# Graph network kernel: four row gathers moved behind four others, and a reciprocal cut into four pieces

## What is computed

```python
h = relu(layernorm(x))                                  # 256 x 1024
feat = concat([h[src], h[dst]], axis=1)                 # per edge, 2048
e_hh = relu(feat[:128] @ W_hh + b_hh)                   # first edges
e_oo = relu(feat[128:768] @ W_oo + b_oo)
e_ho = relu(feat[768:] @ W_ho + b_ho)                   # all other edges
logit = (concat([e_hh, e_oo, e_ho]) @ W_a + b_a)[:, 0]
# softmax of logit over the edges of each dst, then
z = segment_sum(alpha[:, None] * h[src], dst)
x = x + concat([relu([h, z][:64] @ W_hn + b_hn), relu([h, z][64:] @ W_on + b_on)])
# second layer: a 1024 x 1024 matrix, non-zero only in its first 256 x 256
W = zeros(1024, 1024).at[src, dst].add(edge_weight)
return x + relu(layernorm(x)) @ W.T + l1_bias
```

## Time and profile before

| | us |
|---|---|
| median of 3 runs | 326.63 (325.94 to 327.37) |
| profiled execution | 327.02 |
| its span | 325.2 |
| PE busy | 304.7 (94%) |
| DVE busy | 253.2 (78%) |
| ACT busy | 175.9 (54%) |
| POOL busy | 157.0 (48%) |
| DMA | 122.06 MB, mean 375 GB/s |

### The profile page before, as it was taken

How to read it: one execution, slowest core, us unless ns; L and a number is a source line. 1 busy time by engine, 2 the same in 40 slices (tenths; PEclk the granted TensorE clock), 3 DMA queues, 4 the chain that set the end, 5 groups by cost and what they waited for, 6 DMA issues and landing times.

```text
span 325.2 us, 4183 instructions
## 1 busy us (share of the span) xinstructions
PE 304.7 (94%) x1381; PEld 196.4 (60%) x1381; DVE 253.2 (78%) x434; ACT 175.9 (54%) x437; POOL 157.0 (48%) x148
## 2 busy tenths in 40 slices
PE   0899999999999499999999999999999998999995
PEld 0687688845666456656767575666654564366443
DVE  4656445548999199999969989978978979998354
ACT  3854433182467346476884655966219575393202
POOL 3020037405877667757866777538888740000000
PEclk9999999999999969999999999999999999999999
DMA  7999999998999999999999999999999999999604
GB/s 258 406 404 408 366 365 415 409 415 265 342 358 411 410 409 408 410 408 408 411 418 409 409 409 410 408 416 410 408 411 408 410 407 408 408 409 410 231 0 129
DMA packets 34425, 122.06 MB, mean 375 GB/s; under 512 B 4058, under 2 KB 4570, under 8 KB 34404
## 3 DMA queue, kind: packets, MB, share of 16 engines
q0 software_dynamic: 19008, 69.21, 54.1%
q1 hardware_dynamic: 14004, 47.34, 37.6%
q10 hardware_dynamic: 1392, 5.24, 4.0%
HBM read 115.49 MB, written 6.29 MB: 375 GB/s over the span
## 4 chain that ended last, share of the span: by engine, by line
PE 61%; DMA 12%; POOL 11%; DVE 7%; issue 6%; ACT 3%; ACTq 0%; DVEq 0%; POOLq 0%
PE psG L1007 18%; PE psG L865 13%; PE psG L976 9%; DMA Gq<-q_ho,ids 7%; PE psW L915 6%; PE psA L915 5%; POOL Gp L378 5%; POOL Gq L392 5%; DMA q_oo<-T 3%; PE psB L915 3%; PE psG L1084 2%; DVE Gp L681 1%; PE psG L1079 1%; DMA xs<-x 1%; PE psG L876 1%
## 5 line engine op out<-in xcount | busy, mean ns | idle before, releaser
L378 POOL DMA_INDIRECT Gp<-p_ho,ids x60 | 68.2, 1137 | 50.6 <-DMA p_ho<-T 26.3
L392 POOL DMA_INDIRECT Gq<-q_ho,ids x60 | 70.8, 1179 | 34.8 <-issue 17.1
L681 DVE TENSOR_TENSOR Gp<-Gp,Gq 128x1024 f32<-128x1024 f32 x65 | 79.3, 1220 | 10.0 <-DMA Gq<-q_ho,ids 6.8
L1007 PE MATMUL psG<-W,hT 128*128 128x512 f32 x192 | 86.8, 603 | 0.0
L685 DVE SCALAR_TENSOR_TENSOR Gp<-Gp,wa 128x1024 f32<-128x1024 f32 x65 | 79.1, 1217 | 0.4
L1007 PEld LDWEIGHTS psG<-W,hT 128*128 128x128 f32 x192 | 36.2, 194 | 40.2 <-issue 40.2
L489 ACT ACTIVATE RW<-ohs,ewh 128x256 fp32r<-128x256 f32 x66 | 33.2, 503 | 46.8 <-DVE ohs L672 34.4
L915 PE MATMUL psW<-RW,ohd 128*128 128x256 f32 x264 | 44.5, 290 | 1.1 <-issue 1.0
L915 PEld LDWEIGHTS psW<-RW,ohd 128*128 128x128 f32 x264 | 36.3, 189 | 4.5 <-issue 4.3
L915 PE MATMUL psA<-RL,ohd 128*128 128x256 f32 x240 | 35.5, 293 | 3.6 <-issue 2.1
L632 DVE TENSOR_TENSOR Wl<-W,Wh 128x1024 fp32r<-128x1024 f32 x16 | 19.6, 1223 | 21.7 <-ACT Wh L422 21.7
(11 more groups left out here) (180 smaller groups left out, 357.7 us busy)
## 6 DMA issues: line engine op xcount, KB each, us to landing
W<-weights SPq DMA_DIRECT2D x61, 512.0 KB, 13.6
Gp<-weights SPq DMA_DIRECT2D x8, 512.0 KB, 9.9
Gq<-weights SPq DMA_DIRECT2D x4, 512.0 KB, 10.4
pre_f<-weights SPq DMA_DIRECT2D x3, 512.0 KB, 7.9
xs<-x SPq DMA_DIRECT2D x2, 512.0 KB, 3.8
h_rows<-h ACTq DMA_DIRECT2D x1, 1024.0 KB, 6.1
pre_l<-weights SPq DMA_DIRECT2D x2, 512.0 KB, 8.0
p_ho<-T ACTq DMA_DIRECT2D x2, 512.0 KB, 5.4
```

Source lines behind the costliest of these rows:

```text
L378: nc.gpsimd.indirect_dma_start(out=Gp[:, i % NP, :], out_offset=None, in_=p_oo if t <= OO_TILES else p_ho, in_offset=bass.IndirectOffsetOn ...
L392: nc.gpsimd.indirect_dma_start(out=Gq[:, i % NQ, :], out_offset=None, in_=q_oo if t <= OO_TILES else q_ho, in_offset=bass.IndirectOffsetOn ...
L681: nc.vector.tensor_tensor(Gp[:, i % NP, :], Gp[:, i % NP, :], Gq[:, i % NQ, :], ALU.add).then_inc(s_sum, 1)
L1007: last = nc.tensor.matmul(psG[:, 2 * t + half, :], hT[:, k, t * P:(t + 1) * P], W[:, s, half * HALF:(half + 1) * HALF], start=u != 1 and k ...
```

## The change

The order of POOL's first requests was P0 to P11, Q0 to Q7. It becomes P0 to P7, Q0 to Q3, P8 to P11, Q4 to Q7; the rest is as before (Q8, P12, Q9, P13, ...). `few_counts` is no longer called once over 1024 columns ahead of the first row sum; it is called four times, over 256 columns each, after `lot_start(g + 1)` of lots 9, 10, 11 and 12.

```diff
+FEW_LOT = 9
+P_FIRST = 8
@@ gpsimd
-            for i in range(NP):
+            for i in range(P_FIRST):
                 p_rows(i)
-            for i in range(NQ):
+            for i in range(HALVES):
+                q_rows(i)
+            for i in range(P_FIRST, NP):
+                p_rows(i)
+            for i in range(HALVES, NQ):
                 q_rows(i)
             for i in range(NQ, len(GATHERED)):
                 q_rows(i)
@@ vector
-            def few_counts():
+            def few_counts(kind, c):
 
                 dve.wait_ge(s_few, 2)
                 dve.wait_ge(s_wused, SPLIT + 2)
-                chain(nc.vector.tensor_scalar(inv_few[:, :, :, :], few[:, :, :, :], 1.0, None, ALU.max))
-                chain(nc.vector.reciprocal(inv_few[:, :, :, :], inv_few[:, :, :, :]))
-                chain(nc.vector.tensor_scalar(off_few[:, :, :, :], few[:, :, :, :], 0.5, NEG, ALU.is_lt, ALU.mult))
-                chain(nc.vector.tensor_scalar(off_few[:, :, :, :], off_few[:, :, :, :], bar[:, 0:1], None, ALU.add))
+                counts, inverse_of, off_of = few[:, kind, c, :], inv_few[:, kind, c, :], off_few[:, kind, c, :]
+                chain(nc.vector.tensor_scalar(inverse_of, counts, 1.0, None, ALU.max))
+                chain(nc.vector.reciprocal(inverse_of, inverse_of))
+                chain(nc.vector.tensor_scalar(off_of, counts, 0.5, NEG, ALU.is_lt, ALU.mult))
+                chain(nc.vector.tensor_scalar(off_of, off_of, bar[:, 0:1], None, ALU.add))
...
             lot_onehots(0, 0, LOT)
             evac_odd(1)
-            few_counts()
             lot_start(0)
             for g in range(NLOTS):
                 lot_logits(g)
                 lot_start(g + 1)
+                if 0 <= g - FEW_LOT < 2 * NT:
+                    few_counts((g - FEW_LOT) // NT, (g - FEW_LOT) % NT)
```

## The result

The changed kernel takes 331.35 us (median of 4 runs, 329.42 to 332.96), where before takes 327.0 (325.94 to 331.07). The ratio is 1.0126, with a 95% interval of 1.0078 to 1.0174: 4.1 us slower, outside the predicted range. The profiled execution of after took 332.96 us with a span of 331.1. All ratios in this document leave out the executions that fell in a slower state (the traced ones of e10 and e11 among them), and they are formed with executions of before on the same chip, so they need not be the quotient of the two medians.

A forecast was written before the change was run, and what follows sets the result against it. Full DMA engines from about 97 to 301 us were taken as the bound, so the hole before sets the end. Request order +1.3 us and pieces 0, on a median of 326.6, made 327.9 us; range 325.0 to 330.3.

The forecast's parts named there:

- part one: New order of POOL's requests, P8 to P11 behind Q0 to Q3: 1.3 us slower at the end.
- (a): Store of table q_ho lands earlier without P8 to P11 ahead: 3.4 us gained, Q0 asked for at 72.0 us.
- (b): Twelve POOL requests instead of eight ahead of Q8 take 16.3 us: Q8 at 88.3 us, 1.4 us later.
- part two: Counts on DVE in four pieces, 11.8 us added, paid back by its waits: 0 at the end (0 to +3).
- What bounds the kernel: DMA engines full from about 97 to 301 us; the hole before sets the end, if DVE and PE keep up.
- (c): Q8's 1.4 us delay at 369 GB/s leaves 0.52 MB missing, 1.3 us of full DMA to make up behind 97 us.
- (d): DVE's first row sum starts at about 76.7 us, not 80.05; worth nothing, lost in a stop near 114 us.
- The sum: At the end, 1.3 us from the request order and 0 from the pieces: median 327.9 us.
- A: Rival: hole before 97 us filled, Q8 at 85.2 us, 1.7 us earlier; 325.1 us at the end; chance 0.15.
- B: Rival: pieces not paid back, DVE 3 to 4 us late at 262 us; 330.9 us; chance 0.15.
- C: Rival: nothing moves, POOL's gains and losses within 0.5 us; 326.6 us; chance 0.25 together with D.
- D: Rival: PE's slowness around 110 us moves or vanishes; at most some tenths at the end; chance 0.25 with C.

The follow-up runs named there:

- e10: Second set of runs with only POOL's new request order on the kernel before, counts whole at their old place: 329.63 us, ratio 1.0083.
- e11: Kernel before, with P6 to P11 asked for only once the fourth part of the tables has been copied out of PSUM: ratio 1.0007.
- e2: Kernel before with only the counts moved, in four pieces behind lots 9 to 12, old request order: 327.99 us, ratio 1.0035.
- e6: Changed kernel, but with ten P blocks (P0 to P9) ahead of Q0 instead of eight: 329.43 us, ratio 1.0051.
- e9: The changed kernel run again, unchanged: 329.8 us, ratio 1.0111 to the kernel before.
- e5: Changed kernel with the four reciprocals of the counts left out: 330.5 us, ratio 1.0107 to the kernel before.
- e3: Changed kernel, but with only four P blocks (P0 to P3) ahead of Q0: 334.77 us, ratio 1.0279.
- e1: First set of runs with only POOL's new request order on the kernel before, counts whole at their old place: 331.56 us, ratio 1.0176.
- e8: Changed kernel with each of the four reciprocals of the counts made three times: 343.96 us, ratio 1.0494 to the kernel before.
- e4: Kernel before with the counts in four pieces behind lots 14 to 17, old request order: 330.44 us, ratio 1.0121.
- e12: Kernel before with the pieces behind lots 14 to 17 and SP's last four weight loads let go at the 58th row sum, not the 61st: ratio 1.0103.

## Why the prediction was wrong, point by point

The step that failed is the price of part one, and in it two terms: the store's gain (a) and the time of POOL's requests (b). Q8 was to come 1.4 us later and came 3.7 us later; the order was to cost 1.3 us and cost 2.7 and 5.8. The rest of the miss is part two, which was put at 0 and cost 1.1 us.

**What bounds the kernel: right, with its condition.** Behind the hole DMA moves 409 or 410 GB/s on average up to 270 us in every kernel of the table. Behind 280 us some dip (385 GB/s in after, 351 in e2, 359 in e6, over 10 us), where before has 408. The bytes lost ahead of 100 us come back at the end in order and roughly in size, and the number of P blocks in front decides the time. The condition was that DVE and PE keep up. DVE only just does: in after and in e9 it is in the chain that ended last (from 206 and from 175 us), yet 7 us less of its work (e5) changed nothing that can be told.

**(a) The store's gain: mis-sized.** Predicted 3.4 us (2.6 to 5.1), Q0 at 72.0. Measured 2.35 us counted from the store's issue, 2.1 in the time line: Q0 at 73.29, outside the step's bounds. Over all traces of the two orders it is 2.0. The failure was dividing bytes by the full rate. Without P8 to P11 the store doesn't take up the rate that they had; the engines then stand partly empty: 0.71 and 0.29 busy in the two windows from 68 us, 0.09 in the first of them in e3. Why the store can't use them isn't shown. I had read the 10.9 us of the earlier trace rows as a share of the bandwidth "plus some latency" and then priced all of it as bandwidth. 1.3 us of the miss are here.

**(b) POOL's twelve requests: mis-sized.** Predicted 16.3 us, measured 17.3 (17.4 in e9, 16.6 in e1). DVE's first sums began at 78.07 us, beside P8, and from P8's request to the next it took 2.15 us, from P9's 1.66, where I had put 1.42 on average (the requests themselves took 1.84 and 1.36 us); the requests of line 380 and 394 average 1123 and 1199 ns over the whole kernel. Another 1.0 us. The prediction cited what the Trainium skill says of DVE shutting GpSimd out of a port (SBUF — State Buffer, "Who interferes with whom"). The traces agree in kind: of the P and Q requests in all fourteen traces, the 128 with no DVE instruction beside them took 0.93 or 0.94 us, and of the others about half took more than 1 us, up to 2.21. They don't show the 2-port modes as the only cause: nearly all of the long ones stand beside an operation with two input tensors, as the row sums and logits are, and of 46 beside tensor_scalar alone 44 took 0.93 or 0.94 (two took 1.17). Together (a) and (b) put Q8 at 90.59, not at 88.3, 3.7 us later than before and beyond the bound of 2.9.

**(c) What that is at the end: right in kind, and right by its own conversion.** 3.7 us x 369 / 410 = 3.3 us; the windows show 1.3 MB lost, 3.2 us, and the order alone cost 2.7 and 5.8 us. (The prediction's "four requests of 5.2 us" are 16.3 - 11.5 = 4.8 us by its own sum; the forecast used the latter.) Had (a) and (b) been right, the forecast of 1.3 us would have come from the same line. That a stretch of empty DMA engines opened in front of Q0 should have been seen in the earlier trace rows: before, DMA fell to 194 GB/s from 76 to 80 us, though P8 to P11 had been asked for ahead of the store.

**(d) DVE's advance: it was 2.0 us, not 3.3.** That it is worth nothing at the end wasn't tested by itself. The stop near 114 us did not come: PE's slow stretch wasn't there in this execution. It came at 159.13 instead. Here ACT's copy of the first kinds' sums out of PSUM waited 18.20 us (the profile says "remote"; PE fills what it reads, and was in its slow stretch), and behind it in ACT's queue stood the products that free DVE's ring.

**Part two: predicted 0 (0 to +3), measured +1.1 (0.2 to 2.1) in e2.** The pieces took 2.8 us each, not 2.96. That DVE's waits for gathered rows would pay the debt was right in kind (they are gone in after) and a little too generous: 8.1 us of waits stood against 7.9 of debt, without anything to spare, and all of it had to be read from one execution.

**The sum.** Order 2.7 to 3.2 by the lost bytes and pieces 1.1 make 3.8 to 4.3 us; measured were 4.1 and 3.6. The forecast had 1.3 + 0. By the direct measurements the order alone is 2.7 or 5.8, so the sum's closeness is in part luck.

**The rivals.** A (hole filled, 0.15): refuted, Q8 comes 3.7 us later and not earlier. Its second half, Q blocks sped up by P blocks beside them, isn't seen either: 352 and 306 GB/s from 76 to 84 us. B (pieces not paid back, 0.15): true by a third of its size, and the edge that it names is real (e8). C: refuted. D: the slow stretch did move in after's traced execution, which was 2.8 us longer than e9's, where it had not; nothing was gained. The true case was my likeliest mechanism with terms beyond their bounds. I had bounded each by rows of before in which the DMA engines always had other work, and gave "slower" 0.35 though steps (a) and (b) had their uncertainty on one side: the store's gain could not be larger than the bytes allow, but could be as small as nothing.

## What to carry to other kernels

A transfer that others queue behind does not inherit the bandwidth of what is moved out of its way: price its gain from the share that it got in the trace (here about 2 us for 2.1 MB, where the full rate would have made 5.1), and ask what keeps the DMA engines busy until it lands. If the answer is nothing, the moved bytes are lost time in a kernel that is full of transfers later. And work that hides in an early wait is free there; moved into the middle, it seems free only as long as the engine's later waits add up to more than it, and they are soon used up (e2, e4, e8). When one cause of delay is taken away, look for the next wait in the same queue: in e11 it took back a lead of 3 us.

## What the runs showed of the hardware that was not expected

**PE's slow stretch wanders.** In every trace PE's granted clock falls to one half (1.2 GHz) for some microseconds in the middle of the kernel: between 108 and 164 us in most, at 216 us in e1's. In before, after and e9 the matmuls ahead of the fall come singly for some microseconds at a full granted clock, about 0.7 or 1.4 us apart. In after:

```profile
145.50 0.28 PE L923 MATMUL psB<-RL,ohd 128*128 128x256 f32 x1 [1.04 <-issue]
146.22 0.53 PE L923 MATMUL psB<-RL,ohd 128*128 128x256 f32 x2 [0.45 <-issue]
147.64 0.56 PE L923 MATMUL psB<-RL,ohd 128*128 128x256 f32 x1 [0.90 <-issue]
148.00 9.70 PE L1015 MATMUL psG<-W,hT 128*128 128x512 f32 x16
```
```profile
144.00:148.00 4.00, 1.53 (x5) 0.86 (x5) 4.00 (x8) 0.00 (x0) 3.08 (x4) 0.82 1.03 405
148.00:152.00 4.00, 4.00 (x6) 1.71 (x6) 4.00 (x8) 0.00 (x0) 3.39 (x3) 0.50 1.03 410
```

A job of 16 matmuls takes 9.70 us there; elsewhere in the same trace one takes 7.03. The engine was busy 1.53 of 4 us before the clock fell, with its operands ready as far as the profile shows. Before has this at 107 to 115 us, e9 at 107 to 118. In the chain of waits of after it is a piece of 18.18 us under "another core or an unknown queue", and ACT and DVE stood still meanwhile (18.20 and 6.79 us). Whether it costs time at the end isn't settled. DMA was at 405 to 410 GB/s in these windows, which speaks against it; but two of e12's six executions had a mean granted clock of 0.977 and 0.979 and took 332.0 us, and the other four had 0.983 to 0.995 and took 328.0 to 329.5. Its cause is open.

**The first gathers from a table that has just been stored came in below POOL's pace.** In before, the window from 80 us has 289 GB/s, and in e1 the one from 76 us has 299, while the requests of the 4 us ahead were 1.24 to 1.59 us apart; 0.524 MB each 1.59 us would be 330. In after, the 306 GB/s from 80 us fall beside requests 2.15 and 1.66 us apart, which allow 244 and 316, so there the requests may be reason enough. Whether it is, in the other two, the source or the queue's start was not separated.
